# Fetching the high parts of the experts' weights with GpSimd's casting transfers

## The chip, the core and the metric

The kernel runs on one core of one Trainium2 chip. A core has TensorE (matmuls, into PSUM), VectorE and ScalarE (elementwise work), GpSimd, and SyncE, which here only issues DMA transfers. The metric is the device time of one execution in microseconds; the median over the runs is compared.

## The reference

A small vision tower with two layers on 8 images: patch embedding to 64 patches and a class token (65 tokens each, 520 in all) of 192 features, then

```
h = h + attn0(layernorm(h));  h = h + ffn0(layernorm(h))     # 8 experts, 2 chosen per token, hidden 768
h = h + attn1(layernorm(h));  h = h + ffn1(layernorm(h))     # 16 experts, 8 chosen, hidden 128 (8x) or 256 (8x)
```

`attn0` is a polynomial attention, `attn1` an 8-bit fake-quantised one with an integer softmax. In both expert layers the kernel computes all experts for all tokens, and weights the hidden values by the routing weight (zero where an expert isn't chosen):

```
for e in range(NUM_EXPERTS):
    h = gelu(xt @ w1[:, off:off + wd])
    out = out + comb[:, e:e + 1] * (h @ w2[off:off + wd, :])
```

## The kernel before

**Split operands.** The matmuls of the expert layers take operands of type float32r, to which a float32 value has to be rounded. Each float32 operand is therefore split into a high part (the value rounded to float32r) and a low part (the value less the high part), and a product is the sum of three or more products of parts. `fc_hi`, `fc_lo` are the parts of the first weights, `pj_parts` holds both parts of the second ones side by side (columns 0 to 191 high, 192 to 383 low), `hid_hi` and `hid_lo` are those of the hidden values, `xt_hi` and `xt_lo` those of the input.

**Tiles and loads.** Both expert layers go over tiles of 128 hidden units: 48 in the first, 24 in the second. The weights come in 14 loads: loads 0 to 7 of 6 tiles (one expert of the first layer each), loads 8 to 13 of 4 tiles. Each is two transfers, fc (768 or 512 KB) and pj (576 or 384 KB), issued by SyncE into the raw buffers `fc_raw` and `pj_raw`. Raw buffers, `fc_hi`, `fc_lo` and `pj_parts` all have two slots; load n uses slot n % 2.

**Who makes the parts.** For load n there are three pieces: piece 0 and 1 are the two row chunks of fc, piece 2 is pj. ScalarE's `weights_hi` (lines 969 to 977) copies a raw piece into its high part, which rounds it; VectorE's `weights_lo` (lines 1276 to 1286) waits for that and subtracts. The pieces of load n are made in the order of the engines' own instructions behind tiles 0, 1 and 2 of load n - 1 (lines 1000 to 1006 on ScalarE, 1308 to 1312 on VectorE). Piece 2 waits for `pj_mm`, the count of tiles that TensorE has projected, to reach the last tile of load n - 2 (`tiles_to`). Load 0 is made in the first attention layer. SyncE issues the raw transfers of load n when the low parts of load n - 2 are made (`w_lo_done`, lines 460 to 470).

**A tile's way through the engines.** TensorE makes the entry of tile x + 2 (10 matmuls over 260 columns; L597, L642, L644), then the projection of tile x (10 matmuls; L597, L659), and so on with x. ScalarE evicts an entry with gelu (L991), VectorE multiplies by the routing weights (L1301), ScalarE rounds that to `hid_hi` (L998), VectorE subtracts to `hid_lo` (L1306), and each of TensorE's projections waits for `hid_lo` of its tile. All of these are written out in one fixed order per engine:

```
for x in range(len(tiles)):              # TensorE
    if x + 2 < len(tiles):
        for e in entries_of(y, x + 2):
            entry(*e)
    project(x)                           # its last matmul counts pj_mm up
```

GpSimd issues 14 small transfers at the start, sets a few constants, and works in the second attention layer; during the expert layers it does nothing.

Of the kernel before, what the change touches and what calls it, by code (L numbers as in the profile page):

```python
# [29 lines left out]
ACT = mybir.ActivationFunctionType  # L30
# [24 lines left out]
def build(nc, t):  # L55
    with ExitStack() as ctx:
# [175 lines left out]
        wq_in = sem("wq_in")  # L232
        bq_in = sem("bq_in")
        raw_in = [sem(f"raw_in{s}") for s in range(2)]
        w_hi_done = [sem(f"w_hi_done{s}") for s in range(2)]
        w_lo_done = [sem(f"w_lo_done{s}") for s in range(2)]
        dve_done = sem("dve_done")
        act_done = sem("act_done")
# [258 lines left out]
        @block.gpsimd  # L497
        def _(pool):
            pool.dma_start(tok_bias[:], t["tok_bias"].partition_broadcast(128)).then_inc(bias_in, 16)
            pool.dma_start(h[0:B, 4, :], t["cls_tok"].partition_broadcast(B)).then_inc(bias_in, 16)  # L500
            pool.dma_start(ident[:], t["ident"]).then_inc(consts_in, 16)
            pool.dma_start(head_mask[:], t["head_mask"]).then_inc(consts_in, 16)
            pool.dma_start(cls_mask[:], t["cls_mask"]).then_inc(consts_in, 16)
            pool.dma_start(last_mask[:], t["last_mask"]).then_inc(consts_in, 16)
            pool.dma_start(fold[:], t["fold"]).then_inc(consts_in, 16)
            pool.wait_ge(tok_in[TOKK - 1], 16)
            pool.dma_start(wq_raw[:, 0:6, :], t["w_qkv"]).then_inc(wq_in, 16)
            pool.dma_start(wq_raw[:, 6:8, :], t["w_proj"]).then_inc(wq_in, 16)
            pool.dma_start(row_pick[:], t["row_pick"]).then_inc(gates_in, 16)
            pool.dma_start(w_gate0[:], t["w_gate0"]).then_inc(gates_in, 16)  # L510
            pool.dma_start(w_gate1[:], t["w_gate1"]).then_inc(gates_in, 16)
            pool.dma_start(b_qkv[:], t["b_qkv"]).then_inc(bq_in, 16)
            pool.dma_start(b_proj[:], t["b_proj"].partition_broadcast(128)).then_inc(bq_in, 16)

            pool.wait_ge(tok_mm, 4)
            pool.memset(v_pairs[:], 0.0).then_inc(v_zero, 1)
            pool.wait_ge(v_zero, 1)
            for parity in range(2):
                ones = v_pairs[64 * parity:64 * parity + 64, :, parity::2, :, HD:HD + 1]
                pool.memset(ones, 1.0).then_inc(v1_ones, 1)  # L520
            pool.wait_ge(sum_act, 2)
            pool.wait_ge(sum_dve, 2)
            pool.memset(e_last[:], 0.0).then_inc(e_last_zero, 1)

            pool.wait_ge(v_raw_ready, 2)
            own = last_mask[:].unsqueeze(2)
            pool.wait_ge(consts_in, 80)
            for i in range(4):
                for b in range(2):
                    for q in range(2):  # L530
                        pool.tensor_tensor(v_last[:, i, q::2, b, 0:HD], v_raw[:, 2 * i + b], own[:, q::2].broadcast_to([LR, HC, HD]),
                                           ALU.mult).then_inc(v_last_ready, 1)
                pool.tensor_scalar(v_last[:, i, :, :, HD], own.broadcast_to([LR, NH, 2]), 1.0, 0.0, ALU.mult,
                                   ALU.add).then_inc(v_last_ready, 1)

            pool.wait_ge(alpha_ready, 1)
            a, z = CHUNKS[-1]
            pool.tensor_scalar(sc[:, a:z, :], sc[:, a:z, :], col("alpha"), MAGIC, ALU.mult, ALU.add).then_inc(last_t_ready, 1)
            for n, (a, z) in enumerate(CHUNKS[:-1]):
                pool.wait_ge(quot_ready, n + 1)  # L540
                pool.tensor_scalar(pow2[:, a:z, :].bitcast(I32), quot[:, a:z, :], -2.0 ** 23, (127 + OFFSET) * 2.0 ** 23,
                                   ALU.mult, ALU.add).then_inc(pow2_ready, 1)

        @block.tensor
        def _(pe):
# [368 lines left out]
        def _(act):  # L914
# [51 lines left out]
                    act.activation(proj_scale[:, kc * DC:(kc + 1) * DC], PB[4 + kc][:, 4 * DC:5 * DC],  # L966
                                   ACT.Copy).then_inc(wint_t_ready, 1)

            def weights_hi(load, piece):

                s, w = load % 2, LOAD_TILES[load]
                act.wait_ge(raw_in[s], 32 * (load // 2 + 1))
                if piece < 2:
                    ins = act.activation(fc_hi[:, s, piece, 0:w * HT], fc_raw[:, s, piece, 0:w * HT], ACT.Copy)  # L974
                else:
                    ins = act.activation(pj_parts[:, s, 0:w, 0:D], pj_raw[:, s, 0:w, :], ACT.Copy)
                ins.then_inc(w_hi_done[s], 1)

            def ffn(y):

                tiles = TILES[y]

                def entry(kind, x):
                    k = ENTRIES[y].index((kind, x))
                    for n in range(2):
                        act.wait_ge(entry_mm[y], 2 * k + n + 1)
                        src, tok = PB[PAIRS[k % 2][n]][:, 0:HALF], slice(n * HALF, (n + 1) * HALF)
                        if kind == "w":
                            act.activation(tok_w[x % 4][:, tok], src, ACT.Identity).then_inc(entry_out[y], 1)  # L989
                        else:  # L990
                            act.activation(hid[:, x % 2, tok], src, ACT.Gelu_apprx_tanh).then_inc(entry_out[y], 1)  # L991

                def hi_part(x):

                    for n in range(2):
                        act.wait_ge(weighted[y], 2 * x + n + 1)
                        tok = slice(n * HALF, (n + 1) * HALF)
                        act.activation(hid_hi[:, x % 3, tok], hid_w[:, x % 2, tok], ACT.Copy).then_inc(hid_hi_ready[y], 1)  # L998

                def next_weights(x):  # L1000

                    j, load = tiles[x].j, tiles[x].load
                    if j <= 2 and load + 1 < LOADS:
                        if j == 2 and load > E0 * y:
                            act.wait_ge(pj_mm[y], tiles_to(y, load - 1))
                        weights_hi(load + 1, j)

                entry("h", 0)
                comb_turned(y, (E0, E1)[y])
                entry("h", 1)  # L1010
                entry("w", 0)
                for x in range(len(tiles)):
                    if x >= 2:
                        for e in entries_of(y, x):
                            entry(*e)
                    hi_part(x)
                    next_weights(x)

            def comb_turned(layer, n_exp):
                if layer == 0:  # L1020
# [14 lines left out]
            for j in range(KC):  # L1035
                for n in range(2):
                    act.wait_ge(q0_mm, 2 * j + n + 1)
                    act.activation(half(q0, j, n), PB[2 * j + n][0:DC, 0:HALF].rearrange("p (b s) -> p b s", s=S),
                                   ACT.Copy, scale=0.1).then_inc(q0_ready, 1)
            for piece in range(3):  # L1040
                weights_hi(0, piece)
            for g in range(4):
                act.wait_ge(v0_mm, g + 1)
                act.activation(v0[:, 2 * g:2 * g + 2, :], PB[g][0:S, 0:2 * D].rearrange("p (b d) -> p b d", d=D),
# [143 lines left out]
        def _(dve):  # L1188
# [87 lines left out]
            def weights_lo(load, piece):  # L1276

                s, w = load % 2, LOAD_TILES[load]
                dve.wait_ge(w_hi_done[s], 3 * (load // 2) + piece + 1)
                if piece < 2:  # L1280
                    lo, raw, hi = (fc[:, s, piece, 0:w * HT] for fc in (fc_lo, fc_raw, fc_hi))
                    dve.tensor_tensor(lo, raw, hi.bitcast(F32), ALU.subtract).then_inc(w_lo_done[s], 1)  # L1282
# [466 lines left out]
```

## Time and profile before

| | |
|---|---|
| time, median of 3 runs | 371.45 us (371.27 to 372.63) |
| the profiled execution | 371.17 us, of it 369.1 us span |
| first expert layer, entries to sums | about 56 to 178 us |
| second expert layer | about 298 to 360 us |
| busy: TensorE, VectorE, ScalarE, GpSimd | 298.1, 268.8, 202.3, 20.8 us |
| moved by DMA | 27.37 MB |

The span runs from the first to the last instruction that the profiler saw, and the 2 us beside it lie around them. The profile's page gives busy time per engine, strips of 40 slices (9.2 us each) in tenths, the costliest groups of instructions and the transfers. TensorE's time is pipelined: matmuls of 0.28 us start every 0.12 us. What an engine waited for is inferred from semaphores.

### The profile page before, as it was taken

The numbers are of one execution on the slowest core, as the hardware profiler recorded it, in microseconds if no ns is written. First come the engines' busy times: TensorE is split into PE (matmuls) and PEld (weight loads), VectorE is DVE, ScalarE is ACT, GpSimd is POOL, SyncE is SP. The second block draws the span as 40 slices with busy tenths as digits, with TensorE's granted clock in tenths as the row PEclk, the third lists the DMA queues.
The fourth block names the chain that finished last, engine by engine and source line by source line (L and its number), as shares of the span: only waits on it lengthen the run. The fifth ranks groups of instructions, "written<-read, shape, count | busy, mean of one in ns | idle before, by whom it ended". The sixth has DMA issues, their size and how long they took to land.

```text
span 369.1 us, 6068 instructions
## 1 busy us (share of the span) xinstructions
PE 298.1 (81%) x2294; PEld 267.2 (72%) x2294; DVE 268.8 (73%) x717; ACT 202.3 (55%) x486; POOL 20.8 (6%) x46
## 2 busy tenths in 40 slices
PE   5989998899999999999881260099439888999991
PEld 5968857799999999999781140067326278999991
DVE  1269275888888888898668989965468558888852
ACT  1034476677677686777273574660010667777750
POOL 4230000000000000000000015400000000000000
PEclk9999999999999999999996555578557699999997
DMA  6980401235044043000000000000500014444401
GB/s 201 302 275 3 151 0 45 92 133 178 16 166 168 13 151 99 2 1 2 2 0 0 2 2 0 0 2 0 199 0 3 0 33 125 149 154 134 114 7 43
DMA packets 10396, 27.37 MB, mean 74 GB/s; under 512 B 1368, under 2 KB 1992, under 8 KB 10368
## 3 DMA queue, kind: packets, MB, share of 16 engines
q1 hardware_dynamic: 9792, 26.03, 21.9%
q0 software_dynamic: 576, 0.96, 1.2%
q8 instruction: 18, 0.29, 0.3%
q14 instruction: 10, 0.08, 0.1%
HBM read 26.54 MB, written 0.45 MB: 73 GB/s over the span
## 4 chain that ended last, share of the span: by engine, by line
PE 65%; DVE 25%; ACT 5%; issue 2%; DMA 1%; DVEq 0%; ACTq 0%
PE bank L597 26%; PE bank L659 9%; PE bank L577 7%; PE bank L644 4%; PE bank L642 4%; PE bank L700 3%; PE bank L861 2%; PE bank L846 1%; DVE embed_area L1553 1%; ACT hid_hi L998 1%; DVE bn L1204 1%; PE bank L858 1%; DVE group_lo L1508 1%; DVE row_hi L1507 1%; DVE stat_q L1428 1%
## 5 line engine op out<-in xcount | busy, mean ns | idle before, releaser
L597 PE MATMUL bank<-hid_hi,pj_parts 128*128 128x260 f32 x288 | 76.1, 285 | 1.7 <-DVE hid_lo L1306 1.7
L998 ACT ACTIVATE hid_hi<-hidden_area 128x260 fp32r<-128x260 f32 x144 | 55.9, 422 | 38.8 <-DVE hidden_area L1301 37.5
L1306 DVE TENSOR_TENSOR hid_lo<-hidden_area,hid_hi 128x260 fp32r<-128x260 f32 x144 | 56.6, 427 | 10.0 <-ACT hid_hi L998 0.9
L597 PEld LDWEIGHTS bank<-hid_hi,pj_parts 128*128 128x128 f32 x288 | 54.1, 188 | 2.5 <-DVE hid_lo L1306 2.0
L991 ACT ACTIVATE hidden_area<-bank 128x260 f32<-128x260 f32 x144 | 49.2, 377 | 5.7 <-PE bank L644 4.7
L597 PE MATMUL bank<-xt_hi,fc_hi 128*128 128x260 f32 x144 | 41.6, 289 | 1.4 <-ACT hidden_area L989 1.3
L644 PE MATMUL bank<-xt_lo,fc_lo 128*128 128x260 f32 x144 | 41.4, 288 | 0.0
L659 PE MATMUL bank<-hid_hi,pj_parts 128*128 128x260 f32 x144 | 40.7, 283 | 0.0
L659 PE MATMUL bank<-hid_lo,pj_parts 128*128 128x260 f32 x144 | 40.7, 282 | 0.0
L597 PE MATMUL bank<-hid_lo,pj_parts 128*128 128x260 f32 x144 | 40.7, 282 | 0.0
L597 PE MATMUL bank<-xt_lo,fc_hi 128*128 128x260 f32 x144 | 40.7, 282 | 0.0
L642 PE MATMUL bank<-xt_lo,fc_hi 128*128 128x260 f32 x144 | 40.6, 282 | 0.0
L597 PE MATMUL bank<-xt_hi,fc_lo 128*128 128x260 f32 x144 | 40.4, 281 | 0.0
L1301 DVE TENSOR_TENSOR hidden_area<-hidden_area 128x260 f32<-128x260 f32 x72 | 28.0, 424 | 7.0 <-ACT hidden_area L989 6.1
L1301 DVE TENSOR_TENSOR hidden_area<-hidden_area,xn 128x260 f32<-128x260 f32 x72 | 28.1, 423 | 2.2 <-ACT hidden_area L991 1.7
L597 PEld LDWEIGHTS bank<-xt_hi,fc_hi 128*128 128x128 f32 x144 | 27.2, 189 | 1.9 <-ACT hidden_area L989 1.5
L1282 DVE TENSOR_TENSOR fc_lo<-raw_area,fc_hi 128x768 fp32r<-128x768 f32 (+1 forms) x28 | 23.5, 844 | 5.4 <-ACT fc_hi L974 4.3
L597 PEld LDWEIGHTS bank<-hid_lo,pj_parts 128*128 128x128 f32 x144 | 27.3, 190 | 0.0
L597 PEld LDWEIGHTS bank<-xt_lo,fc_hi 128*128 128x128 f32 x144 | 27.1, 189 | 0.1
L597 PEld LDWEIGHTS bank<-xt_hi,fc_lo 128*128 128x128 f32 x144 | 27.1, 188 | 0.0
L659 PEld LDWEIGHTS bank<-hid_lo,pj_parts 128*128 128x128 f32 x144 | 27.1, 188 | 0.0
L659 PEld LDWEIGHTS bank<-hid_hi,pj_parts 128*128 128x128 f32 x144 | 27.1, 188 | 0.0
(299 smaller groups left out, 571.0 us busy)
## 6 DMA issues: line engine op xcount, KB each, us to landing
raw_area<-fc_dram SPq DMA_DIRECT2D x8, 768.0 KB, 4.3
raw_area<-pj_dram SPq DMA_DIRECT2D x8, 576.0 KB, 5.4
xn<-comb_dram SPq DMA_DIRECT2D x12, 260.0 KB, 3.4
raw_area<-fc_dram SPq DMA_DIRECT2D x6, 512.0 KB, 4.1
embed_area<-embed_in_dram SPq DMA_DIRECT2D x8, 352.0 KB, 8.2
hidden_area<-comb_dram SPq DMA_DIRECT2D x9, 260.0 KB, 3.3
raw_area<-pj_dram SPq DMA_DIRECT2D x6, 384.0 KB, 4.4
score_area<-w_l_dram SPq DMA_DIRECT2D x1, 576.0 KB, 11.8
```

The lines of the kernel that those rows point to most:

```text
L577: last = pe.matmul(out, lhs(kc), rhs(kc), start=(kc == 0), stop=(kc == KC - 1))
L597: mm = pe.matmul(out, lhs[a], rhs[b], start=start and n == 0, stop=stop and n == 2, skip_group_check=True)
L642: pe.matmul(out, fc_hi[:, s, 1, cols], x_mix[:, tok], start=False, stop=False, skip_group_check=True)
L644: mm = pe.matmul(out, fc_lo[:, s, 1, cols], x_mix[:, tok], start=False, stop=True, skip_group_check=True)
L659: mm = pe.matmul(PB[SUMS[2 + n]][:, 0:HALF], pj_tails[:, s, j], hidden[:, x % 3, tok], start=x == 0 and part == 0, stop=part == 1, skip_gr ...
L700: mm = pe.matmul(PB[i][:, 0:D], patches[:, k, i * 128:(i + 1) * 128], w_tok[:, k, :], start=(k == 0), stop=(k == TOKK - 1))
L861: last = pe.matmul(PB[4 + i][:, k * 4 * (HD + 1):(k + 1) * 4 * (HD + 1)], e_t[:, HC * i + k, :], v_pairs[:, i, 2 * k:2 * k + 2, :, :].rear ...
L991: act.activation(hid[:, x % 2, tok], src, ACT.Gelu_apprx_tanh).then_inc(entry_out[y], 1)
L998: act.activation(hid_hi[:, x % 3, tok], hid_w[:, x % 2, tok], ACT.Copy).then_inc(hid_hi_ready[y], 1)
L1282: dve.tensor_tensor(lo, raw, hi.bitcast(F32), ALU.subtract).then_inc(w_lo_done[s], 1)
L1301: dve.tensor_tensor(hid_w[:, x % 2, tok], hid[:, x % 2, tok], tok_w[tile.weights][:, tok], ALU.mult).then_inc(weighted[y], 1)
L1306: dve.tensor_tensor(hid_lo[:, x % 3, tok], hid_w[:, x % 2, tok], hid_hi[:, x % 3, tok].bitcast(F32), ALU.subtract).then_inc(hid_lo_ready[y ...
```

## The change

`weights_hi` goes, and with it ScalarE's 42 passes. In their place GpSimd issues two transfers for each load, straight from DRAM into the float32r tensors; the type of the destination makes them casting transfers. SyncE's raw transfers stay as they are, since `weights_lo` still needs the raw values. GpSimd issues loads 0 and 1 at the start, 2 to 9 after its first memsets, and 10 to 13 after its work in the second attention layer. From load 2 on it first waits until TensorE has projected all tiles of load n - 2. `weights_lo` now waits for both raw transfers and for both high transfers of its load, for each of the three pieces.

```diff
+            def high_parts(n):
+
+                s, w, y = n % 2, LOAD_TILES[n], int(n >= E0)
+                if n >= 2:
+                    before = int(n - 2 >= E0)
+                    pool.wait_ge(pj_mm[before], tiles_to(before, n - 2))
+                fc, pj = (t["fc1"][(n - E0 + 2) % 6], t["pj1"][(n - E0 + 2) % 6]) if y else (t["fc0"][n], t["pj0"][n])
+                pool.dma_start(fc_hi[:, s, :, 0:w * HT], fc).then_inc(hi_in[s], 16)
+                pool.dma_start(pj_parts[:, s, 0:w, 0:D], pj).then_inc(hi_in[s], 16)
+
+            for n in range(2):
+                high_parts(n)
             pool.wait_ge(tok_mm, 4)
             pool.memset(v_pairs[:], 0.0).then_inc(v_zero, 1)
...
+            for n in range(2, E0 + 2):
+                high_parts(n)
             pool.wait_ge(sum_act, 2)
             pool.wait_ge(sum_dve, 2)
             pool.memset(e_last[:], 0.0).then_inc(e_last_zero, 1)
...
+            for n in range(E0 + 2, LOADS):
+                high_parts(n)
...
-            def weights_hi(load, piece):
-
-                s, w = load % 2, LOAD_TILES[load]
-                act.wait_ge(raw_in[s], 32 * (load // 2 + 1))
-                if piece < 2:
-                    ins = act.activation(fc_hi[:, s, piece, 0:w * HT], fc_raw[:, s, piece, 0:w * HT], ACT.Copy)
-                else:
-                    ins = act.activation(pj_parts[:, s, 0:w, 0:D], pj_raw[:, s, 0:w, :], ACT.Copy)
-                ins.then_inc(w_hi_done[s], 1)
-
...
-                def next_weights(x):
-
-                    j, load = tiles[x].j, tiles[x].load
-                    if j <= 2 and load + 1 < LOADS:
-                        if j == 2 and load > E0 * y:
-                            act.wait_ge(pj_mm[y], tiles_to(y, load - 1))
-                        weights_hi(load + 1, j)
-
...
-            for piece in range(3):
-                weights_hi(0, piece)
...
             def weights_lo(load, piece):
 
                 s, w = load % 2, LOAD_TILES[load]
-                dve.wait_ge(w_hi_done[s], 3 * (load // 2) + piece + 1)
+                dve.wait_ge(raw_in[s], 32 * (load // 2 + 1))
+                dve.wait_ge(hi_in[s], 32 * (load // 2 + 1))
```

## Rows read from the trace of the kernel before

**Rows 1.** The page's strips, 40 slices of 9.2 us: granted clock in tenths, GB/s moved.

```profile
PEclk9999999999999999999996555578557699999997
GB/s 201 302 275 3 151 0 45 92 133 178 16 166 168 13 151 99 2 1 2 2 0 0 2 2 0 0 2 0 199 0 3 0 33 125 149 154 134 114 7 43
```

**Rows 2.** Window: length, busy (instructions) of PE, PEld, DVE, ACT, POOL; clock, DMA share, GB/s.

```profile
78.00:92.00 14.00, 14.00 (x119) 14.00 (x117) 11.90 (x28) 10.16 (x28) 0.00 (x0) 1.00 0.34 117
```

**Rows 3.** L974, L976: ScalarE's busy time; L1282, L1285: VectorE's idle time, times.

```profile
0.00:369.10 369.10, 20.58 (x28) 0.88 0.23 74
0.00:369.10 369.10, 14.19 (x14) 0.88 0.23 74
ACT fc_hi L974: 4.3, 14
ACT pj_parts L976: 7.0, 13
```

**Rows 4.** Timeline of TensorE and VectorE, load 0: start, us, what, idle before.

```profile
63.68 0.96 DVE L1282 TENSOR_TENSOR fc_lo<-raw_area,fc_hi 128x768 fp32r<-128x768 f32 x1 [0.30 <-ACT fc_hi L974]
...
69.72 1.43 DVE L1285 TENSOR_TENSOR pj_parts<-raw_area,pj_parts 128x768 fp32r<-128x768 f32 x2 [0.63 <-ACT pj_parts L976]
...
71.98 0.77 DVE L1306 TENSOR_TENSOR hid_lo<-hidden_area,hid_hi 128x260 fp32r<-128x260 f32 x2
72.46 0.39 PE L597 MATMUL bank<-hid_hi,pj_parts 128*128 128x260 f32 x1 [0.98 <-DVE hid_lo L1306]
```

**Rows 5.** Timeline of both engines where load 0 ends and load 1 begins.

```profile
77.86 0.96 DVE L1282 TENSOR_TENSOR fc_lo<-raw_area,fc_hi 128x768 fp32r<-128x768 f32 x1 [0.31 <-ACT fc_hi L974]
78.47 0.28 PE L659 MATMUL bank<-hid_lo,pj_parts 128*128 128x260 f32 x1
79.64 0.77 DVE L1306 TENSOR_TENSOR hid_lo<-hidden_area,hid_hi 128x260 fp32r<-128x260 f32 x2
82.21 0.28 PE L597 MATMUL bank<-hid_hi,pj_parts 128*128 128x260 f32 x1
```

**Rows 6.** The same at the end of load 8, in the second layer.

```profile
313.57 0.69 DVE L1282 TENSOR_TENSOR fc_lo<-raw_area,fc_hi 128x512 fp32r<-128x512 f32 x1
313.94 0.28 PE L659 MATMUL bank<-hid_lo,pj_parts 128*128 128x260 f32 x1
317.67 0.29 PE L597 MATMUL bank<-hid_hi,pj_parts 128*128 128x260 f32 x1
```

**Rows 7.** DMA issues around 128 and 142 us: KB, us from issue to landing.

```profile
raw_area<-pj_dram SPq DMA_DIRECT2D x1, 576.0 KB, 5.3
raw_area<-pj_dram SPq DMA_DIRECT2D x1, 384.0 KB, 4.3
```

**Rows 8.** The page's DMA queues: packets, MB, share of 16 engines.

```profile
q1 hardware_dynamic: 9792, 26.03, 21.9%
q0 software_dynamic: 576, 0.96, 1.2%
```

**Rows 9.** Timeline: one issue of GpSimd, VectorE after load 0's low parts, SyncE's fc issues.

```profile
19.06 0.54 POOL L513 DMA_DIRECT2D b_proj<-b_proj_dram  x1
...
38.33 0.42 DVE L1407 SCALAR_TENSOR_TENSOR attn_area<-attn_area 65x260 f32<-65x260 f32 x1 [1.49 <-ACT attn_area L1048]
...
128.25 0.33 SPq L443 DMA_DIRECT2D raw_area<-fc_dram  x1
...
142.74 0.70 SPq L443 DMA_DIRECT2D raw_area<-fc_dram  x1
```

**Rows 10.** Windows of TensorE: length, busy (instructions), granted clock, DMA share, GB/s.

```profile
194.80:197.00 2.20, 0.00 (x0) 0.99 0.00 0
197.00:200.00 3.00, 0.92 (x3) 0.50 0.00 0
239.50:244.50 5.00, 5.00 (x25) 0.50 0.00 0
245.00:246.00 1.00, 1.00 (x8) 1.00 0.00 0
```

More of the change, by code:

```diff
@@ L234, in build @@
         raw_in = [sem(f"raw_in{s}") for s in range(2)]
-        w_hi_done = [sem(f"w_hi_done{s}") for s in range(2)]
+        hi_in = [sem(f"hi_in{s}") for s in range(2)]
         w_lo_done = [sem(f"w_lo_done{s}") for s in range(2)]
@@ L1016, in ffn @@
                     hi_part(x)
-                    next_weights(x)
             def comb_turned(layer, n_exp):
```

## The prediction

> **What bounds the kernel now.** I read the page's strips first, then the windows of each stage, the waits, and last the timelines around one change of weights. The clock's strip [rows 1] tells the stages apart: full through the first expert stage (about 62 to 177 us), half or little more through most of the second attention, full again in the second expert stage (302 to 360 us). In a window of the first expert stage TensorE is busy for all 14 us, VectorE for 11.9 and ScalarE for 10.2 [rows 2]. So ScalarE, whose passes over the weights are the thing removed, is not the bound in the expert stages. The 42 passes cost 20.6 + 14.2 = 34.8 us of ScalarE [rows 3], but what counts is who waits for them: VectorE, 11.3 us in all [rows 3], and TensorE waits for VectorE hardly at all. The one place where it does is the first load, where VectorE has no lead yet: TensorE sits idle before the projections of tiles 1, 2 and 3, 1.0 us before the last of them [rows 4].
>
> How a load changes is in [rows 5]. Done with tile 0 of load 1, VectorE turns to the low part of load 2's first piece: it waits 0.31 us for ScalarE and starts at 77.86. TensorE at that time is projecting the last tile of load 0: that ends at 78.47 + 0.28 = 78.75. It projects tile 1 of load 1 at 82.21. VectorE is thus about one tile ahead, and this lead is what hides it.
>
> **The change, part by part.** *Removed:* the ScalarE passes. In steady state nobody on TensorE's path gains, because the windows have no idle TensorE time [rows 2]. In load 0 VectorE's waits for ScalarE go, twice 0.30 and once 0.63 us, and TensorE's idle time shrinks with them [rows 4]: by 0.6 us before tile 3 and by some 0.2 us each before tiles 1 and 2, 1.0 us gained. In the first attention stage the three passes of load 0 lie before a ScalarE wait for TensorE, so nothing.
>
> *Added wait:* this is the main thing. Before, the raw transfer of load n was issued two loads ahead into a buffer of its own, and the first two ScalarE passes of load n needed no wait for the projections of load n-2. Now `high_parts(n)` writes fc_hi and pj_parts of load n together, so GpSimd waits for `pj_mm` of the last tile of load n-2, and only then issues the first of the two transfers. VectorE's `weights_lo(n, 0)` needs both transfers (`hi_in` at 32 per load), and stands in VectorE's order behind tile 0 of load n-1. By [rows 5] it gets there at 77.6, that is 1.2 us *before* the transfer can even be issued (78.75). The wait therefore holds the whole time of the fetch, call it L. Behind it on VectorE stand the weighting and the low part of tile 1, hence ScalarE's `hid_hi` of that tile, hence TensorE's projection of tile 1. TensorE has only the entries of tiles 2 and 3 and the projection of tile 0 to do meanwhile: up to 82.21, 3.46 us after 78.75.
>
> After landing, VectorE takes 1.78 us from the start of `fc_lo` to the start of `hid_lo` (77.86 to 79.64), and TensorE starts 0.48 us after that start (71.98 to 72.46) [rows 4, 5]. So TensorE stands still for L + 1.78 + 0.48 - 3.46 = L - 1.2 us. In the second stage TensorE's reserve is the same, from 313.94 + 0.28 = 314.22 to 317.67, 3.45 us, and VectorE's step is 0.27 shorter, as its `fc_lo` takes 0.69 us in place of 0.96 [rows 5, 6]: 1.51 + 0.48 - 3.45, so L - 1.5.
>
> *How many:* loads 2 to 8 are caught in the first stage (7), loads 10 to 13 in the second (4). Loads 0 and 1 are fetched at the start, and load 9 has the whole second attention.
>
> *How long is L?* No transfer of this form is in the trace: it has no casting one. A floor is SP's plain transfers of the same bytes, alone on the queues: the second, issued some 0.4 us behind the first, takes 5.3 us, so 5.7 us; for the small loads 0.7 + 4.3 = 5.0 us [rows 7, 9]. A software price comes from the queue lines: GpSimd's queue moved 0.96 MB in 1.2% of 369.1 us, 217 GB/s, SP's 26.03 MB in 21.9%, 322 GB/s [rows 8]. For 1.38 MB that is 6.3 against 4.3 us, 2.1 more (rounded); for 0.92 MB 1.4 more. GpSimd's issue takes 0.54 us where SyncE's takes 0.33 [rows 9]: 0.3 more for two, and I add 0.4 for its start from a semaphore, my choice. That gives L = 5.7 + 2.1 + 0.7 = 8.5 us. In the second stage 5.0 + 1.4 + 0.7 = 7.1, and I add 0.4 for sharing, since the raw transfers and comb rows already move 114 to 154 GB/s in that stage [rows 1]: 7.5 us. Standstills: 7.3 us and 6.0 us. The ceiling is a cast that halves the software rate (108 GB/s): L = 14.9 and 11.7 us. I take the software rate, the row nearest in kind.
>
> The Trainium skill ("DMA: Bandwidth & Descriptors", Anatomy of one DMA) fits a GpSimd-issued transfer as 2.0 us plus its bytes at 436 GB/s. Taken for the pair that would be, as an estimate, 5.2 and 4.1 us, and the whole sum would come to about 434 us. Its § SWDGE vs HWDGE vs iDMA says that a float32r destination always counts as a cast and has to come from GpSimd, and names no rate for one.
>
> *The clock:* TensorE has been at the full level through every expert window. Elsewhere it went to half (1.2 GHz) once it had stood idle from 194.8 to 197; on resuming at 239.5 it stayed at half for 5 us of busy time before it rose [rows 10]. Standstills of 6 to 7 us are longer than that idle time, so I let every one of the 11 end at half level. The same work takes half as long at full, so 5 us cost 2.5; I take 2.3, since part of it runs where TensorE would wait for VectorE's next pieces anyway. Bounds: 0 and 2.5.
>
> *Start-up:* the transfers of loads 0 and 1 (2.75 MB) are issued from 19.6 us on, behind b_proj [rows 9]. What was in flight is through by slice 4, 27.7 us, in which almost nothing moves [rows 1]. Even if load 0 got nothing before that, it would land at 27.7 + 6.3 = 34.0. VectorE is idle for 1.49 us up to 38.33 [rows 9] behind load 0's low parts (2 x 0.96 + 1.43 = 3.35 us [rows 4]), so it comes to them at 33.5 and has until 35.0. Nothing, and up to 4 us at the ceiling rate. `wq_raw` and the gates are issued ahead of them.
>
> *Moved:* GpSimd's own compute work stays between the same waits. The memset of `e_last` comes behind `high_parts(9)`, whose `pj_mm` wait ends no later than its own. SP's later raw loads and comb rows start later with VectorE and stay early enough.
>
> *The sum:* 7 x (7.3 + 2.3) = 67.2; 4 x (6.0 + 2.3) = 33.2; less 1.0: +99 us. The profiled execution took 371.17 us (span 369.1 and 2.1 around it), 0.3 us below the median of 371.45, so about 470 us.
>
> **The rivals.** (a) *The cast costs nothing and the transfers move like SP's*, L = 5.7 and 5.0. With the clock's loss this is 7 x 6.8 + 4 x 5.8 - 1.0 = +70, 441 us; with the clock kept, 7 x 4.5 + 4 x 3.5 - 1.0 = +44, 416 us. For it: small rows did not slow SP's transfers [rows 7]. Against: the software queue's lower rate [rows 8]. Chance 0.17.
>
> (b) *The cast halves the software rate.* 7 x (13.7 + 2.3) + 4 x (10.2 + 2.3) + 2 (start-up) - 1.0 = +163, 534 us. For it: every word is converted on the way, and nothing in the trace speaks against it. Chance 0.24.
>
> (c) *The fetch is hidden*, the other side: the wait ends within TensorE's reserve. It decides at L = 1.2 us; then only the 1.0 us of load 0 remains, 370 us. It would need 1.38 MB to land in a quarter of what the fastest row gives, or GpSimd to be released earlier than [rows 5] say. Chance 0.03.
>
> (d) *The change does nothing measurable*, because VectorE reaches the wait later than I think and the fetch cost lies in its idle time. VectorE's idle time in the window is 2.1 of 14 us [rows 2], so it can't take 7. Chance 0.01.
>
> **How the numbers follow.** The forecast has 0.55, (a) 0.17, (b) 0.24, (c) and (d) 0.04. The range goes from between the two figures of (a) to just past (b): 425 to 545 us. A difference of 0.5% (1.9 us) is about what a measurement can tell. Slower by more than that: 0.96; within: 0.02; faster: 0.02.
>
> **What would show it.** In the changed profile VectorE's `fc_lo` (line of `weights_lo`) should wait for the DMA into fc_hi or pj_parts 11 times, 9 to 10 us each in the first stage, and TensorE should wait for `hid_lo` at the second tile of loads 1 to 7 and 9 to 12, 7 and 6 us each. Its granted clock should fall to half in each of these loads. GpSimd's queue should carry 17.5 MB (8 x 1.38 + 6 x 0.92 = 16.5, and the old 0.96). Load 0 should show smaller idle times before tiles 1 to 3. I am wrong if the fetch is not late, if it lands in under 5 or over 15 us, or if the clock stays up.

## The result, and the profile after

The changed kernel takes 447.37 us (median of 4 runs, 447.06 to 449.02), the kernel before beside it on the same chip 371.36 (4 runs, 370.55 to 372.63): 1.205 times as long, with a 95% interval of 1.201 to 1.210. The forecast was 470, range 425 to 545. Ratios here and below compare undisturbed runs of both kernels alone, so they can differ a little from the quotient of the medians.

The page of the changed kernel: clock strip, DMA queues, and of the costliest groups the one that TensorE's standstill lies before, and VectorE's first pieces.

```profile
PEclk9969999989798979697989855569558998886998
...
q1 hardware_dynamic: 9792, 26.03, 17.7%
q0 software_dynamic: 12800, 17.48, 15.4%
...
L613 PE MATMUL bank<-hid_hi,pj_parts 128*128 128x260 f32 x288 | 86.3, 316 | 54.7 <-DVE hid_lo L1302 54.7
...
L1278 DVE TENSOR_TENSOR fc_lo<-raw_area,fc_hi 128x768 fp32r<-128x768 f32 (+1 forms) x28 | 23.4, 840 | 89.1 <-DMA pj_parts<-pj_dram 89.1
```

The strip [rows 1] was full through the first expert stage; now it has a dent for nearly every load. GpSimd's queue carries 17.48 MB, as forecast. Its rate while busy is 17.48 MB in 15.4% of the span of 445.2 us, 255 GB/s, where the 0.96 MB of [rows 8] gave 217; SP's queue by the same working gives 330.

The waits of VectorE and of TensorE in the first expert stage (57 to 225 us), and the same two in the second (370 to 440): what waited, for what, us in total, times, longest.

```profile
DVE fc_lo L1278 <- DMA pj_parts<-pj_dram: 59.6, 7, 9.2
PE bank L613 <- DVE hid_lo L1302: 38.3, 9, 6.1
...
DVE fc_lo L1278 <- DMA pj_parts<-pj_dram: 29.5, 4, 8.1
PE bank L613 <- DVE hid_lo L1302: 16.4, 4, 4.4
```

VectorE waits seven and four times, at the loads that the prediction named. TensorE's first row has two waits more, 0.6 us together, which are load 0's; the other 11 come to 54.1 us. One of them in full, the timeline where load 0 ends and load 2 is fetched (to be read against [rows 5]):

```profile
81.11 0.28 PE L675 MATMUL bank<-hid_lo,pj_parts 128*128 128x260 f32 x1
...
81.70 0.54 POOL L522 DMA_DIRECT2D fc_hi<-fc_dram  x1 [57.37 <-PE bank L675]
82.23 0.83 POOL L523 DMA_DIRECT2D pj_parts<-pj_dram  x1
88.04 0.96 DVE L1278 TENSOR_TENSOR fc_lo<-raw_area,fc_hi 128x768 fp32r<-128x768 f32 x1 [7.86 <-DMA pj_parts<-pj_dram]
...
90.31 0.58 PE L613 MATMUL bank<-hid_hi,pj_parts 128*128 128x260 f32 x1 [5.30 <-DVE hid_lo L1302]
```

and the windows behind the end of TensorE's wait (TensorE's busy time second, the clock third from the end):

```profile
90.30:93.00 2.70, 2.69 (x12) 2.70 (x13) 2.55 (x7) 1.55 (x6) 0.00 (x0) 0.50 0.00 0
...
93.40:96.00 2.60, 2.60 (x24) 2.60 (x23) 2.45 (x7) 1.23 (x4) 0.00 (x0) 1.00 0.31 47
```

The last tile's projection ends at 81.11 + 0.28 = 81.39, GpSimd begins to issue at 81.70, and VectorE goes on at 88.04. The fetch takes 6.3 us from the issue; L, which the prediction counts from the end of the projection, is 6.6. TensorE has stood still for 5.30 us when it goes on at 90.31, at half clock for some 3 us, 12 matmuls in 2.7 us where 24 fit into 2.6 at the full clock. The clock falls to half at each of the other ten standstills too, the shortest of them 3.9 us, in it or within 0.6 us of its end.

Read in the same way for all 11 loads, L is 6.6 to 7.4 us for the six of 768 and 576 KB (mean 7.0), and 5.6 to 6.0 for the five of 512 and 384 KB (mean 5.7; loads 8 and 10 to 13). The standstill is L - 1.35 in each of the six and L - 1.6 in each of the five.

**Where the 76.1 us of span went.** The stages can be cut at the same instructions in both kernels: the first expert tile, the last transposition behind that stage, the first tile of the second layer's experts. Windows (length, then TensorE's busy time with its matmuls; the clock stands third from the end), before:

```profile
61.59:178.44 116.85, 114.37 (x941) 113.36 (x940) 97.52 (x226) 84.74 (x216) 0.00 (x0) 1.00 0.25 84
178.44:302.16 123.72, 70.90 (x508) 51.17 (x509) 90.57 (x263) 51.18 (x101) 11.15 (x25) 0.67 0.05 16
302.16:369.10 66.94, 58.28 (x479) 57.40 (x478) 50.14 (x121) 42.27 (x112) 0.00 (x0) 0.96 0.35 104
```

and after:

```profile
65.73:233.71 167.98, 128.88 (x940) 126.80 (x940) 96.76 (x226) 66.88 (x192) 10.10 (x15) 0.89 0.37 113
233.71:353.52 119.81, 66.83 (x508) 49.11 (x509) 90.92 (x263) 51.19 (x101) 12.12 (x27) 0.70 0.08 24
353.52:445.20 91.68, 67.34 (x479) 65.63 (x478) 48.97 (x121) 33.60 (x97) 5.90 (x8) 0.87 0.41 116
```

- Standstill: 38.3 + 16.4 = 54.7 us, less the 1.7 that TensorE waited for `hid_lo` in the same stage before: +53.0.
- Clock: the same 940 matmuls are busy for 128.88 us in place of 114.37, the 479 of the second layer for 67.34 in place of 58.28. That is 14.5 + 9.1 = +23.6 us, 2.1 for each of the 11 loads.
- Start: the first expert tile comes at 65.73 in place of 61.59: +4.1.
- The second attention stage, which the change doesn't touch, is 3.9 us *shorter* (119.81 for 123.72), with TensorE's busy time 4.1 shorter for the same 508 matmuls: its clock rose at another moment.

These make 76.8, 0.7 more than the 76.1.

### The profile page after: what moved, and what is told of

Its sections match the earlier page's. It is cut to its first block, busy times and chain, and to the rows that moved or that the text cites. A ratio compares the mean times of both kernels' runs of the same rounds, so it can differ in the third digit from the quotient of the medians.

```text
span 445.2 us, 6074 instructions
## 1 busy us (share of the span) xinstructions
PE 320.7 (72%) x2294; PEld 288.2 (65%) x2294; DVE 268.5 (60%) x717; ACT 173.3 (39%) x444; POOL 40.5 (9%) x74
## 3 DMA queue, kind: packets, MB, share of 16 engines
q0 software_dynamic: 12800, 17.48, 15.4%
## 4 chain that ended last, share of the span: by engine, by line
PE 47%; DVE 25%; DMA 16%; ACT 4%; issue 3%; POOL 2%; SPq 1%; DVEq 0%; ACTq 0%
PE bank L613 20%; DMA pj_parts<-pj_dram 13%; PE bank L675 7%; PE bank L593 6%; PE bank L660 3%; PE bank L658 3%; DVE fc_lo L1278 3%; DMA embed_area<-embed_in_dram 2%; ACT hid_hi L1004 2%; PE bank L877 2%; DVE hid_lo L1302 2%; POOL fc_hi L522 2%; DVE hidden_area L1297 1%; DVE embed_area L1549 1%; DVE bn L1199 1%
## 5 line engine op out<-in xcount | busy, mean ns | idle before, releaser
L613 PE MATMUL bank<-hid_hi,pj_parts 128*128 128x260 f32 x288 | 86.3, 316 | 54.7 <-DVE hid_lo L1302 54.7
L613 PEld LDWEIGHTS bank<-hid_hi,pj_parts 128*128 128x128 f32 x288 | 61.7, 214 | 57.4 <-DVE hid_lo L1302 56.9
L613 PE MATMUL bank<-xt_hi,fc_hi 128*128 128x260 f32 x144 | 44.0, 306 | 0.9 <-ACT hidden_area L995 0.6
L613 PE MATMUL bank<-hid_lo,pj_parts 128*128 128x260 f32 x144 | 44.5, 309 | 0.0
L675 PE MATMUL bank<-hid_hi,pj_parts 128*128 128x260 f32 x144 | 44.2, 307 | 0.0
L675 PE MATMUL bank<-hid_lo,pj_parts 128*128 128x260 f32 x144 | 44.0, 306 | 0.0
L613 PE MATMUL bank<-xt_lo,fc_hi 128*128 128x260 f32 x144 | 43.1, 299 | 0.0
L613 PE MATMUL bank<-xt_hi,fc_lo 128*128 128x260 f32 x144 | 42.8, 297 | 0.0
L658 PE MATMUL bank<-xt_lo,fc_hi 128*128 128x260 f32 x144 | 42.7, 296 | 0.0
L522 POOL DMA_DIRECT2D fc_hi<-fc_dram x14 | 8.6, 616 | 315.9 <-PE bank L675 315.9
L613 PEld LDWEIGHTS bank<-hid_lo,pj_parts 128*128 128x128 f32 x144 | 31.2, 217 | 0.0
L675 PEld LDWEIGHTS bank<-hid_hi,pj_parts 128*128 128x128 f32 x144 | 31.0, 215 | 0.0
L613 PEld LDWEIGHTS bank<-xt_hi,fc_hi 128*128 128x128 f32 x144 | 30.0, 208 | 1.3 <-ACT hidden_area L995 0.8
L675 PEld LDWEIGHTS bank<-hid_lo,pj_parts 128*128 128x128 f32 x144 | 30.7, 213 | 0.0
L613 PEld LDWEIGHTS bank<-xt_lo,fc_hi 128*128 128x128 f32 x144 | 29.7, 206 | 0.1
```

The costliest lines, as they stand in the source:

```text
L522: pool.dma_start(fc_hi[:, s, :, 0:w * HT], fc).then_inc(hi_in[s], 16)
L613: mm = pe.matmul(out, lhs[a], rhs[b], start=start and n == 0, stop=stop and n == 2, skip_group_check=True)
L658: pe.matmul(out, fc_hi[:, s, 1, cols], x_mix[:, tok], start=False, stop=False, skip_group_check=True)
L675: mm = pe.matmul(PB[SUMS[2 + n]][:, 0:HALF], pj_tails[:, s, j], hidden[:, x % 3, tok], start=x == 0 and part == 0, stop=part == 1, skip_gr ...
```

## The experiments

**1. The start.** The prediction put nothing here; the trace shows 4.1 us. VectorE and GpSimd in the changed kernel's start (timeline: start, us, what):

```profile
19.55 0.17 DVE L1210 TENSOR_SCALAR var_eps<-mv 128x5 f32<-128x5 f32 x1
19.60 0.55 POOL L522 DMA_DIRECT2D fc_hi<-fc_dram  x1
...
20.86 3.34 DVE L1221 TENSOR_SCALAR xn<-h,mv,rstd 128x192 f32<-128x192 f32 x3
...
22.32 1.48 POOL L528 MEMSET embed_area<- 128x1632 f32 x1
```

and in the kernel before:

```profile
19.54 1.55 DVE L1215 TENSOR_SCALAR var_eps<-mv 128x5 f32<-128x5 f32 x1
...
22.04 0.94 DVE L1226 TENSOR_SCALAR xn<-h,mv,rstd 128x192 f32<-128x192 f32 x3
```

The three `xn` passes take 3.34 us in place of 0.94, while GpSimd issues and then runs its memset; before, a five-column pass takes 1.55 us in place of 0.17. Windows on the `xn` line alone (length, VectorE's busy time with its passes) tell the passes of the changed kernel apart:

```profile
21.20:21.60 0.40, 0.40 (x1) 1.00 1.03 273
21.60:22.00 0.40, 0.40 (x1) 1.00 1.26 317
22.00:22.40 0.40, 0.40 (x2) 1.00 0.83 219
```

One pass fills the time from 20.86 to beyond 22.0, beside the two issues of load 1 and before the memset has begun; it takes some 1.4 to 1.5 us. The second, beside the memset, takes 1.6, and the third 0.36. Alone, each takes 0.37. So is it the memset or the issues? The first experiment puts the first four issues behind the memsets:

```diff
-            for n in range(2):
-                high_parts(n)
             pool.wait_ge(tok_mm, 4)
...
-            for n in range(2, E0 + 2):
+            for n in range(E0 + 2):
                 high_parts(n)
```

> The changed kernel with one thing moved: GpSimd issues the transfers of loads 0 and 1 behind its memsets of v_pairs instead of ahead of them. In the changed kernel the first expert layer begins 4.1 us later than before, and VectorE's three normalising passes took 3.3 us instead of 0.9 while GpSimd was at its issues and its memset. Theory A, the big memset alone holds VectorE up: it is back at its old place, the 4.1 us go, 443.3 us. Theory B, GpSimd's issues of large transfers hold VectorE up too: the passes now meet the issues, and at least half of the delay stays, 445 to 447.5 us. Theory C, the early transfers themselves (2.75 MB more on the queues) are what is late: no change, 447.4 us, with VectorE's passes at 0.9 us.

Measured: 1.199 times before (1.188 to 1.209), median 447.59 with runs from 443.36 to 452.77. The two shortest, 443.36 and 444.46, lie near theory A's 443.3, but with that spread the time alone settles nothing. VectorE in its timeline:

```profile
19.54 1.15 DVE L1208 TENSOR_SCALAR var_eps<-mv 128x5 f32<-128x5 f32 x1
...
21.64 1.12 DVE L1219 TENSOR_SCALAR xn<-h,mv,rstd 128x192 f32<-128x192 f32 x3
...
61.20 0.87 DVE L1295 TENSOR_TENSOR hidden_area<-hidden_area 128x260 f32<-128x260 f32 x2 [3.04 <-ACT hidden_area L993]
```

The hold-up beside the memset has moved with it, back to `var_eps`, and the first expert tile stands at 61.20. The issues, which lie beside the `xn` passes here too, cost these 0.2 us only. In the changed kernel one pass beside them took over 1 us more, and the `xn` totals of 3.2 to 3.4 us in all seven kernels of this study with that order say the same. So about half of the 2.4 us lies beside the memset and half beside the issues, and an issue doesn't always hold a pass. Which moment of the issue does it was not tested.

The control is the kernel before with this edit alone:

```diff
-            pool.wait_ge(tok_mm, 4)
+            pool.wait_ge(xt_mm, NT)
             pool.memset(v_pairs[:], 0.0).then_inc(v_zero, 1)
```

> The kernel before with one edit: GpSimd's 128x1632 memset waits for the last of the first transposes (some 24 us) in place of the token matmul (19 us). Theory A, that this memset holds VectorE's passes while both run: var_eps takes 0.17 us in place of 1.55 and the time falls by about 1.4 us (0.994 to 0.998 of before). Rival B, that VectorE was held by something else in the 1.55 us: var_eps stays at 1.5 us and the time is the same.

Measured: 370.75 us, 0.997 (0.993 to 1.000); one of the 12 runs took 1000.42 us and is left out of the ratio. In its timeline `var_eps` is short and the first tile comes 0.84 us earlier than at 61.59:

```profile
19.31 0.17 DVE L1215 TENSOR_SCALAR var_eps<-mv 128x5 f32<-128x5 f32 x1
...
60.75 0.87 DVE L1301 TENSOR_TENSOR hidden_area<-hidden_area 128x260 f32<-128x260 f32 x2 [3.04 <-ACT hidden_area L989]
```

For the memset the mechanism is shown, by this run alone; its worth by the first tile, 0.8 us, is smaller than the expected 1.4. The Trainium skill ("SBUF — State Buffer", Who interferes with whom) says that VectorE's copies and tensor_scalar passes in a two-port mode and GpSimd's instructions lock each other out for the whole instruction; the 1.55 us beside a 1.48 us memset agree with the whole length.

But a hold-up of 2.4 us in `xn` need not be 4.1. Seven kernels of this study have the changed kernel's order at the start, with 3.2 to 3.4 us of `xn`. In five (those of experiments 2 and 3, and below the version with early waits, its repeat and the one with eight added transfers) the granted clock is full in the window 25 to 31.6 us, and the first tile comes at 61.95 to 62.86. In the changed kernel and the one with late separate waits the clock is at half in that window, and the tile comes at 65.73 and 68.54. So the hold-up costs 0.4 to 1.3 us, and 3 to 6 more where the clock falls over it. What decides whether it falls was not settled.

**2. The clock's share.** TensorE is kept busy during the wait with matmuls of zeros into a bank that the next ones accumulate into:

```diff
+                    if tiles[x].j == 1 and (1 <= tiles[x].load <= 7 or 9 <= tiles[x].load < LOADS - 1):
+                        for _ in range(34):
+                            pe.matmul(PB[5][:, 0:HALF], zeros[:, 0:128], zeros[:], start=False, stop=True,
+                                      skip_group_check=True)
                     project(x)
```

> The changed kernel with 34 matmuls of zeros (some 4.1 us at full clock), which add zero to a sum bank, ahead of the projection of the second tile of each of the 11 loads that stand still. They fill the standstill and lengthen nothing else. Theory A, the granted clock falls because TensorE stands idle, and each fall costs some 1.6 us of work at half speed: the clock stays full and the time falls by some 15 us, to 430 to 435 us, with the waits for hid_lo shrunk by what the zeros take. Theory B, the clock costs nothing, since TensorE has to wait for VectorE's next tiles anyway: 447 us or a little more.

Measured: 435.06 us (433.23 to 439.62), 1.177 times before (1.164 to 1.190), 12 us below the changed kernel and at the upper end of the 430 to 435 expected. Windows of its two expert stages, and from its timeline the 34 matmuls once:

```profile
62.83:223.90 161.07, 147.02 (x1178) 139.88 (x1178) 95.29 (x226) 64.72 (x192) 10.12 (x15) 0.98 0.39 118
...
347.66:434.40 86.74, 74.41 (x615) 70.54 (x614) 48.59 (x121) 32.51 (x97) 5.91 (x8) 0.98 0.45 123
```

```profile
81.97 3.94 PE L691 MATMUL bank<-zeros 128*128 128x260 bf16 x34
```

Take the zero matmuls off (7 and 4 times 3.94 us) and the real ones are busy for 119.4 and 58.7 us, against 128.88 and 67.34: 18 of the 23.6 us of clock loss are gone. The two stages become 11.9 us shorter, not 18, because the fill (43.3 us) and what is left of the waits (17.4) last 6 us longer than the old waits did (54.7). So the idle time is what costs the clock, and most of the term goes with it; filling it buys back half.

**3. The fetch, moved by 1.5 us.** GpSimd runs a memset of 1.47 us between its wait and the first issue, in loads 2 to 13:

```diff
                     pool.wait_ge(pj_mm[before], tiles_to(before, n - 2))
+                    if n == 2:
+                        pool.wait_ge(v1_ones, 2)
+                    pool.memset(scratch[:], 0.0).then_inc(pause, 1)
+                    pool.wait_ge(pause, n - 1)
```

> The changed kernel with a GpSimd memset of a scratch buffer (128 x 1632, 1.5 us by the profile) between the wait for pj_mm and the first issue, for each of loads 2 to 13. Theory A, the fetch's time enters one for one 11 times (load 9 has time): +1.5 to 1.7 us each, +16 to +19 us, 464 to 467 us. Theory B, part of the fetch is still hidden or something else ends the wait: clearly less than +12 us.

Measured: 462.74 us (462.34 to 463.2), 1.250 times before (1.244 to 1.255): 15.4 us more than the changed kernel, 1.4 for each of 11 loads, and just under the 464 to 467 expected. TensorE's first wait grows from 5.30 to 6.96 us:

```profile
88.42 0.58 PE L619 MATMUL bank<-hid_hi,pj_parts 128*128 128x260 f32 x1 [6.96 <-DVE hid_lo L1308]
```

What is added to L comes out one for one: in this kernel too the standstill is L - 1.35 in each of the six large loads and L - 1.6 in the five small ones. Nothing hides any of it.

**4. What makes the fetch late: one common wait, or the late issue?** First, a semaphore for each part, both still issued behind the projection of the last tile of load n-2:

```diff
-                pool.dma_start(fc_hi[:, s, :, 0:w * HT], fc).then_inc(hi_in[s], 16)
-                pool.dma_start(pj_parts[:, s, 0:w, 0:D], pj).then_inc(hi_in[s], 16)
+                pool.dma_start(fc_hi[:, s, :, 0:w * HT], fc).then_inc(fc_in[s], 16)
+                pool.dma_start(pj_parts[:, s, 0:w, 0:D], pj).then_inc(pj_in[s], 16)
...
-                dve.wait_ge(hi_in[s], 32 * (load // 2 + 1))
+                dve.wait_ge((fc_in if piece < 2 else pj_in)[s], 16 * (load // 2 + 1))
```

> The changed kernel with one semaphore for each of the two parts, both still issued behind the projection of the last tile: tells the worth of separate waits from that of the early issue. Theory A (the early issue does it): the first part is ready at its own landing, about 5.1 us behind the wait in place of 6.3 in the large loads and 4.6 in place of 5.1 in the small, so 10 us less standstill in all and the clock about as before: 432 to 440 us. Rival B (the common semaphore is what holds): the standstill falls under 15 us and the time under 395.

Measured: 428.47 us (426.36 to 431.73), 1.152 times before (1.145 to 1.159). That is 19 us less than the changed kernel, some 4 below the range of theory A and far above that of B. Its groups and its timeline:

```profile
L614 PE MATMUL bank<-hid_hi,pj_parts 128*128 128x260 f32 x288 | 84.3, 311 | 37.1 <-DVE hid_lo L1303 37.1
```

```profile
84.51 0.54 POOL L523 DMA_DIRECT2D fc_hi<-fc_dram  x1 [60.41 <-PE bank L676]
...
89.24 0.96 DVE L1279 TENSOR_TENSOR fc_lo<-raw_area,fc_hi 128x768 fp32r<-128x768 f32 x1 [6.25 <-DMA fc_hi<-fc_dram]
```

VectorE now goes on 4.7 us after GpSimd's release, not 5.1: the expectation had added the issue of the second transfer to that of the first. Counted from the end of the projection, L is now 5.0 us in the six large loads and 4.5 in the five small ones. The prediction's formula, L - 1.2 and L - 1.5, gives 6 x 3.8 + 5 x 3.0 = 37.8 us; the 11 standstills measure 36.3, again L - 1.35 and L - 1.6 each (the 37.1 of the page have 0.8 of three short waits in them). The common semaphore was worth a quarter of the loss. The rest is left to the place of the issue, which the next run moves.

Then the early issue too. fc_hi is last read by the entry of the last tile of load n-2, pj_parts by its projection, and each part now waits for its own reader (in addition to the edits above):

```diff
                 if n >= 2:
-                    before = int(n - 2 >= E0)
-                    pool.wait_ge(pj_mm[before], tiles_to(before, n - 2))
+                    last = tiles_to(before, n - 2) - 1
+                    pool.wait_ge(entry_mm[before], 2 * ENTRIES[before].index(("h", last)) + 2)
...
                 pool.dma_start(fc_hi[:, s, :, 0:w * HT], fc).then_inc(fc_in[s], 16)
+                if n >= 2:
+                    pool.wait_ge(pj_mm[before], tiles_to(before, n - 2))
```

> The changed kernel with the wait split: the fc transfer of load n waits only for the entry of the last tile of load n-2 (the last reader of fc_hi), the pj transfer for the projection as before; VectorE's pieces 0 and 1 wait for fc alone, piece 2 for pj alone. Theory A, the cost is the late start of the fetch, one for one: fc is issued some 3.7 us earlier and needs 5.1 us instead of 6.3, so it lands 80.2 us where 77.9 is wanted; TensorE's standstill per load falls from 5.4 us to 0 to 1 us and the clock stays at the full level: 376 to 386 us. Theory B, it is the casting traffic or GpSimd's descriptor work that slows VectorE or the queues: nearly as slow as now, 430 us or more.

Measured: 369.31 us (366.81 to 375.55, 10 runs), 0.995 times before (0.991 to 0.999), below the 376 to 386 of theory A. Timeline, and the window of its first expert stage:

```profile
71.92 0.54 POOL L524 DMA_DIRECT2D fc_hi<-fc_dram  x1 [47.67 <-PE bank L664]
...
78.41 0.96 DVE L1282 TENSOR_TENSOR fc_lo<-raw_area,fc_hi 128x768 fp32r<-128x768 f32 x1 [1.43 <-DMA fc_hi<-fc_dram]
78.50 0.83 POOL L527 DMA_DIRECT2D pj_parts<-pj_dram  x1 [6.04 <-PE bank L679]
```

```profile
62.52:177.89 115.37, 114.03 (x941) 113.37 (x941) 95.72 (x226) 65.59 (x192) 10.87 (x16) 1.00 0.55 169
```

The first part is issued 6.6 us ahead of the second, where the expectation had counted on 3.7. VectorE still waits for it, 8.2 us in 6 times, but its lead covers that: TensorE waits 0.6 us for `hid_lo` in the whole span, and in the first expert stage the clock stays full. All of the loss has gone, although every byte and every cast is as in the changed kernel. The first expert stage is 1.5 us shorter than before. Of this 1.1 is TensorE's wait for `hid_lo` in load 0, 0.6 us for 1.7: the gain that the prediction put at 1.0.

**5. Is the cast slow?** In the version with early waits GpSimd issues, in the second attention stage, eight transfers one behind the other: 768 KB of fc cast, the same plain, 576 KB of pj cast, the same plain, and all again. They put load 2's weights over the low parts of load 8, which VectorE has worked out by then, so the output is not that of the reference.

```diff
+            for dst, src in 2 * [(fc_lo[:, 0], fc2), (fc_raw[:, 0], fc2), (pj_parts[:, 0, 0:T0, D:], pj2), (flat, pj2)]:
+                n += 1
+                pool.dma_start(dst, src).then_inc(probe, 16)
+                pool.wait_ge(probe, 16 * n)
             pool.wait_ge(v_raw_ready, 2)
```

> The version with separate, early waits, and behind GpSimd's memset of e_last, where no other transfer runs, eight transfers one behind the other, twice each: the 768 KB of fc cast, the same plain into an f32 tile, the 576 KB of pj cast into the strided high halves' layout, the same plain into a dense tile. It measures what a cast adds to a transfer of GpSimd's queue. Theory A, that a cast costs little: the cast fc lands within 0.5 us of the plain one, both at 3.5 to 5 us from issue, and the cast pj within 1 us of the plain one. Rival B, that the cast sets the 6.3 us which a pair took in the changed kernel: each cast transfer takes over 1.5 us longer than its plain one. The time of the whole rises by the 35 us that the eight take, less what GpSimd waits for there anyway; it is not compared.

Its timeline of GpSimd; in brackets the wait for the transfer before:

```profile
178.51 0.54 POOL L549 DMA_DIRECT2D fc_lo<-fc_dram  x1
184.84 0.54 POOL L549 DMA_DIRECT2D raw_area<-fc_dram  x1 [5.79 <-DMA fc_lo<-fc_dram]
189.57 0.83 POOL L549 DMA_DIRECT2D pj_parts<-pj_dram  x1 [4.18 <-DMA raw_area<-fc_dram]
194.29 0.54 POOL L549 DMA_DIRECT2D raw_area<-pj_dram  x1 [3.89 <-DMA pj_parts<-pj_dram]
198.56 0.53 POOL L549 DMA_DIRECT2D fc_lo<-fc_dram  x1 [3.73 <-DMA raw_area<-pj_dram]
203.59 0.53 POOL L549 DMA_DIRECT2D raw_area<-fc_dram  x1 [4.50 <-DMA fc_lo<-fc_dram]
208.47 1.09 POOL L549 DMA_DIRECT2D pj_parts<-pj_dram  x1 [4.34 <-DMA raw_area<-fc_dram]
213.52 0.54 POOL L549 DMA_DIRECT2D raw_area<-pj_dram  x1 [3.96 <-DMA pj_parts<-pj_dram]
```

and, from its transfers, pj cast and pj plain, us from issue to landing, the median of two:

```profile
pj_parts<-pj_dram POOLq DMA_DIRECT2D x2, 576.0 KB, 4.6
raw_area<-pj_dram POOLq DMA_DIRECT2D x2, 576.0 KB, 4.5
```

From issue to issue: fc cast 6.33 (with load 9's last part still in flight beside it) and 5.03, fc plain 4.73 and 4.88; pj cast 4.72 and 5.05, pj plain 4.27 for the one that another transfer follows. So a cast costs a GpSimd transfer between 0.2 and 0.8 us by this count, and by the landings of pj 0.1, with two draws of each and a different layout of the target in the pj pair. It does not cost half the rate. The 6.3 us and more of a pair in the changed kernel are then not the cast's: alone, each part lands within 4.8 us of its issue. The whole took 367.48 us in its one run, so the eight were hidden.

**6. A better version.** The early waits, and at the start one mend or both: the first fetches behind the memsets, which stay in their place (the first edit of experiment 1), or fetches and memsets behind the last of the first transposes (both edits).

> Separate, early waits for the two parts, and the first two fetches behind GpSimd's memsets. Theory A: the separate waits alone put the first tile of the expert layer at 62.5 us and the span at 365; with the memsets first the tile stands at 61.2 as it did with that order alone, so about 1.3 us less than with the separate waits alone: 0.983 to 0.993 of before, 365 to 369 us. Rival B, that the first fetches' place doesn't matter once TensorE's clock stays up in the start: equal to the separate waits alone, 0.993 to 0.999.

> Separate, early waits, and GpSimd's memsets and the first two fetches behind the last of the first transposes, so that VectorE runs its statistics and its xn passes alone. Theory A: xn x3 at 0.94 us and var_eps at 0.17, the expert layer's first tile at 59.8 to 60.3 us and the time 1.3 us below that of the version with the memsets only first: 363 to 367 us, 0.978 to 0.989 of before. Rival B, that the first fetches (issued 6 us later, landing beside the scale reductions of the weights) come late for load 0 or hold VectorE's passes at 26 to 31 us: no gain over the version with the memsets first, or a wait for the fc_hi transfer in front of load 0's first piece.

Measured on one chip: 369.29 us for the first (0.997, 0.992 to 1.002; 0.983 to 0.993 was expected), 367.95 for the second (0.990, 0.985 to 0.995; 0.978 to 0.989 was expected). The second in its timeline:

```profile
20.75 0.94 DVE L1223 TENSOR_SCALAR xn<-h,mv,rstd 128x192 f32<-128x192 f32 x3
...
60.88 0.87 DVE L1299 TENSOR_TENSOR hidden_area<-hidden_area 128x260 f32<-128x260 f32 x2 [3.04 <-ACT hidden_area L997]
62.59 0.95 DVE L1280 TENSOR_TENSOR fc_lo<-raw_area,fc_hi 128x768 fp32r<-128x768 f32 x1
```

Load 0's first piece doesn't wait, and the first tile comes at 60.88, later than the 59.8 to 60.3 expected. The quiet start and the waits alone were run once more side by side:

> The version with separate, early waits and GpSimd's memsets and first fetches behind the first transposes, again, beside the one with the waits alone on the same chip: 0.985 to 0.995 of before, and 1 to 2.5 us below the one with the waits alone if the start is worth what the first tile's place says (60.9 in place of 62.5 us).

> The version with separate, early waits alone, again: 0.991 to 0.999 of before. If it comes out level with the one with the quiet start, the 1.6 us of the first tile's place are lost again in the attention stage, whose clock rises at another moment.

Measured: 369.45 us, 0.994 (0.989 to 0.999), and 371.95 us, 1.001 (0.996 to 1.006), where 0.991 to 0.999 was expected. So the early waits alone are level with the kernel before, 0.995 once and 1.001 once. With the quiet start the kernel is faster than before both times, by 1.0 and 0.6%, 2 to 4 us. Its lead over the waits alone, some 0.6%, is within the intervals, and the traces hardly show it: the last transposition of the first expert stage comes at 177.95 and 177.41 us with the quiet start, and at 177.89 without. Most of the first tile's 1.6 us is thus lost again before the attention stage begins. With the quiet start VectorE waits 12.1 us for `fc_hi` in that stage in place of 8.2, and TensorE's 941 matmuls are busy for 1.3 us more; why was not followed. Single runs of each kernel spread over some 10 us, more than any of these differences.

## Why the prediction was right, point by point

- *The added wait holds the whole fetch, and TensorE stands still for L - 1.2 and L - 1.5:* right. Measured, it is L - 1.35 in the large loads and L - 1.6 in the small ones, in each of 33 loads of the changed kernel and of experiments 3 and 4, in which L goes from 4.3 to 8.6 us.
- *How many:* 7 and 4, right. But load 8, the last of the seven, has the 512 and 384 KB of the second stage, and was priced like the other six: 7.3 us of standstill, where its own terms (7.1 - 1.5) give 5.6 and 3.95 were measured.
- *L = 8.5 and 7.5 us:* the term that was mis-sized. Measured: 7.0 and 5.7 us on the mean. The step that failed is what the prediction laid on its floor of 5.7 and 5.0 us, SP's plain transfers. It added a software price of 2.1 and 1.4 us, 0.3 for GpSimd's slower issues, 0.4 for the start, and in the second stage 0.4 for sharing. The start takes 0.3. The fetch from its issue takes 6.7 and 5.4 us, so that 1.0 and 0.4 are left for all the rest. The software price came from the rates of [rows 8]. With those of the changed kernel's page, 255 against 330 GB/s, the same arithmetic gives 1.2 and 0.8. So 217 GB/s, read from 0.96 MB in small transfers, was too low for large ones. The estimate from the Trainium skill ("DMA: Bandwidth & Descriptors", Anatomy of one DMA), 5.2 and 4.1 us, is 1.5 and 1.3 us below the 6.7 and 5.4; the measurement decides.
- *Clock, 2.3 us for each load:* right, 2.1 measured.
- *Start-up, nothing:* wrong, 4.1 us. The prediction asked only when the transfers land, and held that GpSimd's own work stays between the same waits. But four issues now stand ahead of its memset, which begins at 22.32 in place of 19.59, and the prediction didn't ask what VectorE does then. The memset fell from a five-column pass onto an `xn` pass, the issues onto another, and in this kernel TensorE's clock fell behind that.
- *Load 0, 1.0 us gained:* right. TensorE's waits for `hid_lo` in it go from 1.7 to 0.6 us, 1.1 less.
- *The sum:* the measured parts 53.0 + 23.6 + 4.1 - 3.9 = 76.8, against +99. The standstills were put at 7 x 7.3 + 4 x 6.0 = 75.1 and measure 54.1, 21 us less: 10 for the six large loads, 3 for load 8, 8 for the other four. The clock's term was 1.7 us too high. The 4.1 of the start and the -3.9 of the attention stage, neither in the sum, cancelled by chance.
- *The rivals:* (a), the cast costs nothing and the clock is lost, said 441. As a statement of the fetch's time it was nearer than the forecast: from its issue the fetch lies 1.0 and 0.4 us above the floor. (b) is refuted by experiment 5 and by L itself (14.9 and 11.7 us were its terms), (c) and (d) by the waits.

## What to carry to other kernels

A transfer that waits for a buffer costs its whole time, less the small reserve of the engines behind it (here 1.35 of 7.0 us), when its reader stands ahead of the release. So split the release by part, and wait for the last reader of each: here that took 447 us back to 370 without moving a byte less. Before costing a moved wait by bandwidth, ask for the time of a transfer from rows of its size, and don't take a rate from a queue that only carried small ones. After a move on GpSimd, look at which VectorE instructions now lie beside its memsets and its issues.

## What the runs showed that was not expected

- A write-only memset of 1.48 us on GpSimd holds VectorE's f32 tensor_scalar passes for its whole length, down to one of 5 columns (1.55 us for 0.17). Beside GpSimd's transfer issues a pass of 0.37 us took over 1.4 us in the changed kernel, while in experiment 1 four issues cost three such passes 0.2 us in all.
- Alone, a casting transfer takes 0.1 to 0.8 us more than a plain one of the same queue. A pair of them moved 372 GB/s in the window 84 to 87 us of the changed kernel, in which no other transfer was issued.
- The same 508 matmuls of the attention stage were busy for 66.8 to 70.9 us in profiles of kernels that don't differ there: the moment at which the clock rises is worth 4 us, as much as most of the smaller edits here. A stage-by-stage cut is then more telling than the time of the whole.
- TensorE's clock fell to half in or just behind each of the 11 standstills of 3.9 to 6.1 us. In the load shown it stayed there for 3 us of work; by the stage windows this cost 2.1 us for each load.
